# A fused attention and mixture-of-experts block on eight cores: the expert weight loads wait for named tensors of the stage before in place of a fence, and four input loads are recorded earlier

## The chip, the cores and the metric

The kernel runs on the eight cores of one Trainium2 chip. Each core works on one batch element of x (2048 tokens of width 1024) with the same program and its own copy of all weights to read; no core sends anything to another. The metric is the device time of the slowest core in microseconds (us), lower is better.

## The reference, cut to what matters

One layer: x is normalised (layer norm without weights), and three things are added to it: an attention block with its feed-forward part, and a block of eight experts with a router.

```python
xn = layernorm(x)
x = x + attn_block(xn) + expert_block(xn)

def attn_block(x):            # x is xn
    xi = rmsnorm(x @ down_w + down_b, norm1_w)          # 1024 -> 512, two branches of 256
    o1 = branch(xi[..., :256], window=10, shift=5)      # windowed attention, 8 heads each
    o2 = branch(xi[..., 256:], window=20, shift=10)
    x = x + concat(o1, o2) @ up_w + up_b
    h = rmsnorm(x, norm2_w)
    return x + gelu(h @ ffn_w1 + ffn_b1) @ ffn_w2 + ffn_b2   # 1024 -> 2048 -> 1024

def expert_block(t):          # t is xn
    logits = silu(t @ rw1 + rb1) @ rw2 + rb2            # 8 logits
    w = softmax over the two largest logits, 0 elsewhere
    eh = silu(einsum('td,edh->teh', t, ew1) + eb1)      # every expert on every token
    eo = einsum('teh,ehd->ted', eh, ew2) + eb2
    return t + einsum('te,ted->td', w, eo)
```

All eight experts are computed for all tokens: `ew1` is 8 x 1024 x 2048 and `ew2` 8 x 2048 x 1024 in float32, 128 MiB in all, and each core reads all of it.

## The kernel before, in words

**How the order is set.** A class `Prog` (L34) records operations into one list per engine (tensor, vector, scalar, gpsimd, sync). Each operation names the resources (`Res`, L26) it reads and writes, and `op` (L50) derives its semaphore waits from them: a read waits for the tokens of the resource's writers (`w`), a write for those of its writers and of its readers (`rs`). An engine's own list is its order; the order in which operations of different engines are recorded matters only for which tokens exist when a wait is derived. The book-keeping of a write is the part that the change leans on:

```python
for w in wr:
    if w.rs:
        w.w = [tok]
        w.rs = []
    else:
        w.w.append(tok)
```

So a second write of a resource that nobody has read in between waits for the first write, and its token is added to the list. For a DMA the token is its landing: each DMA has a semaphore name (`dma=`) that rises by 16 when it has landed. `fence` (L94) makes the next operation of each engine wait for everything recorded so far on all engines.

**The stages**, each with its own SBUF tensors, opened and closed in turn, so that a later stage's tensors lie where an earlier stage's were:

- P0 (L290 to L362): 16 tiles of 128 tokens of x, each through six small steps `u0` to `u5` (load by SyncE, statistics by VectorE, two ScalarE steps, normalise and start the sum S, eight transposes, copy into XN), recorded in a staggered order by `step` and `sidx` (L354 to L359). The load `u0` (L310) goes to one of four buffers `XST`.
- Router (L364 to L480), attention branches (L482 to L843).
- A4 (L845 to L1034): up projection, norm and feed-forward, two blocks of 512 tokens at a time. `a4_ffn1` (matmuls L962) fills `MID`, `a4_ffn2` (matmuls L987, bias matmul L991) multiplies by `WF2` into PSUM, and VectorE adds the result to the running sum S (L999, L1007). Then comes `P.fence()` (L1032).
- Experts (L1037 to L1133): for each expert e, the weights come as eight DMAs that GpSimd issues, float32 in HBM to bf16 in SBUF, each 1 MiB as it is written: four column quarters of the first matrix into `WE1` (L1066, semaphores `de1` + slot + quarter) and four row quarters of the second into `WE2` (L1071, semaphores `de2` + quarter). `WE1` has two slots (e % 2), `WE2` one. For each block `nt` of 512 tokens, 16 groups of eight matmuls (L1079) make the hidden values, ScalarE applies Silu (L1086) into `EHS`, and for each of four token tiles 16 matmuls `blds_lo` and 16 `blds_hi` (L1098) give the output, which VectorE scales and adds to S (L1116). `blds_lo` reads the quarters 0 and 1 of `WE2`, `blds_hi` 2 and 3. The group m of L1079 reads quarter m // 4 of `WE1`.

`EB2R` is a small tensor (16 KiB) with the experts' output bias; its DMA (L1042) is the first that GpSimd issues after the fence, and the 12 loads of expert 0's `WE1`, `WE2` and of expert 1's `WE1` follow it, with no wait between them. PE reads tokens block by block in order, so nothing of expert 0 past its first `blds_hi` runs before all eight of its loads have landed.

Of the kernel before, what the change touches and what calls it, by code (L numbers as in the profile page):

```python
# [17 lines left out]
NTC = 16  # L18
# [193 lines left out]
def build_nc():  # L212
    nc = bass.Bass("TRN2", target_bir_lowering=False)
    es = ExitStack()
    P = Prog(nc, es)
    t_, v_, s_, g_, y_ = nc.tensor, nc.vector, nc.scalar, nc.gpsimd, nc.sync
# [3 lines left out]
    CN = {}  # L220
# [31 lines left out]
    rFB2R, rEB2R = Res("FB2R"), Res("EB2R")  # L252
# [12 lines left out]
    blk_cm = nc.Block()  # L265
    blk = blk_cm.__enter__()

    for n in CS:
        P.op("sync", (lambda d=CS[n], a=CN[n].ap(): y_.dma_start(d[:, :], a)),
             wr=[rCS[n]], dma="dc_" + n)  # L270
    for n in BRANCH_CONSTS:
        rCS[n] = Res(n)
    P.op("gpsimd", (lambda: g_.dma_start(FB2R[:, :], CN["fb2"].ap())),
         wr=[rFB2R], dma="dcg1")
# [20 lines left out]
    if True:  # L295
        rPT = rPBF
        rXST = [Res(f"XST{i}") for i in range(4)]
        rXNT = [Res(f"XNT{i}") for i in range(4)]
        rMV4 = [Res(f"MV4{i}") for i in range(4)]

        def p0_stages(tc):
            p4 = tc % 4
            p2 = tc % 2
            xs = XST[:, 1024 * p4: 1024 * p4 + 1024]
            xnt = XNT[:, 1024 * p4: 1024 * p4 + 1024]
            mv = MV4[:, 16 * p4: 16 * p4 + 16]
            rmv = rMV4[p4]

            def u0():
                P.op("sync", (lambda tc=tc, xs=xs: y_.dma_start(  # L310
                    xs, xd.ap()[128 * tc: 128 * tc + 128, :])),
                    wr=[rXST[p4]], dma=f"dx{p4}")

            def u1():
                P.op("vector", (lambda: v_.bn_stats(mv[:, 0:6], xs[:, 0:512])),
                     rd=[rXST[p4]], wr=[rmv])
                P.op("vector", (lambda: v_.bn_stats(mv[:, 6:12], xs[:, 512:1024])),
                     rd=[rXST[p4]], wr=[rmv])
                P.op("vector", (lambda: v_.bn_aggr(mv[:, 12:14], mv[:, 0:12])),
                     rd=[rmv], wr=[rmv])  # L320

            def u2():
                P.op("scalar", (lambda: s_.activation(mv[:, 14:15], mv[:, 13:14],
                                                      AF.Ln, bias=CS["epsc"][:, 0:1])),
                     rd=[rmv, rCS["epsc"]], wr=[rmv])
                P.op("scalar", (lambda: s_.activation(mv[:, 15:16], mv[:, 14:15],
                                                      AF.Exp, scale=-0.5)),
                     rd=[rmv], wr=[rmv])

            def u3():  # L330
                P.op("vector", (lambda: v_.tensor_scalar(  # L331
                    xnt, xs, mv[:, 12:13], mv[:, 15:16], ALU.subtract, ALU.mult)),
                    rd=[rXST[p4], rmv], wr=[rXNT[p4]])
                P.op("vector", (lambda tc=tc: v_.tensor_tensor(
                    S[:, 1024 * tc: 1024 * tc + 1024], xs, xnt, ALU.add)),
                    rd=[rXST[p4], rXNT[p4]], wr=[rS[tc]])

            def u4():
                for fc in range(8):
                    P.op("tensor", (lambda fc=fc: t_.transpose(  # L340
                        PT[:, 1024 * p2 + 128 * fc: 1024 * p2 + 128 * fc + 128],
                        xnt[:, 128 * fc: 128 * fc + 128], CS["idb"][:, :])),
                        rd=[rXNT[p4], rCS["idb"]], wr=[rPT[p2]])

            def u5():
                P.op("scalar", (lambda tc=tc: s_.copy(
                    XN3[:, :, 128 * tc: 128 * tc + 128],
                    PT[:, 1024 * p2: 1024 * p2 + 1024].rearrange(
                        "p (c x) -> p c x", c=8))),
                    rd=[rPT[p2]], wr=[rXN4[tc // 4]])  # L350

            return [u0, u1, u2, u3, u4, u5]

        p0s = [p0_stages(tc) for tc in range(NTC)]  # L354
        for step in range(NTC + 5):
            for sidx in range(6):
                t = step - sidx
                if 0 <= t < NTC:
                    p0s[t][sidx]()  # L359
        P.fence()  # L360
        P.replay(blk)
# [123 lines left out]
    if True:  # L485
        rUPIN = [Res(f"UPIN{i}") for i in range(NNT)]
        rWUP = Res("WUP")
# [27 lines left out]
        for n in BRANCH_CONSTS:  # L515
# [3 lines left out]
                 wr=[rCS[n]], dma="dc_" + n)  # L519
        if True:  # L520
# [22 lines left out]
            if True:  # L543
# [17 lines left out]
                for c in range(4):  # L561
                    P.op("vector", (lambda c=c: v_.memset(XI3[:, c, 2048:2052], 0.0)),
                         wr=[rXI])
# [35 lines left out]
            if True:  # L599
# [109 lines left out]
                for br in range(2):  # L709
# [67 lines left out]
                    for step in range(17 + NSTG - 1):  # L777
                        for sidx in range(NSTG):
                            t = step - sidx
# [76 lines left out]
        if True:  # L856
            rH = [Res("H0"), Res("H1")]
            rMID = Res("MID")
            rRST2 = Res("RST2")
            rWF1, rWF2 = Res("WF1"), Res("WF2")  # L860
# [155 lines left out]
            for pr in range(2):  # L1016
# [12 lines left out]
                a4_ffn2(n0)  # L1029
                a4_ffn1(n1)  # L1030
                a4_ffn2(n1)
            P.fence()  # L1032
            P.replay(blk)
        esA4.close()  # L1034
    esU.close()
# [3 lines left out]
    EB2R = esM.enter_context(nc.sbuf_tensor("EB2R", [8, 1024], BF16))  # L1039
    rOST = [Res("OST0"), Res("OST1")]  # L1040
    WE1 = esM.enter_context(nc.sbuf_tensor("WE1", [128, 2 * 8 * 2048], BF16))
    _ = P.op("gpsimd", (lambda: g_.dma_start(EB2R[:, :], CN["eb2"].ap())),  # L1042
             wr=[rEB2R], dma="dcg2")
    WE2 = esM.enter_context(nc.sbuf_tensor("WE2", [128, 16 * 1024], BF16))
    EHS = esM.enter_context(nc.sbuf_tensor("EHS", [128, 16 * 512], BF16))
    PA, PB = Fb(0), Fb(1)
# [2 lines left out]
    if True:  # L1049
        rWE1Q = [[Res(f"we1_{sl}_{q}") for q in range(4)] for sl in range(2)]  # L1050
        rWE2Q = [Res(f"we2_{q}") for q in range(4)]
# [8 lines left out]
        e1hbm = CN["e1w"].ap().rearrange("e (k p) m -> e p k m", p=128)  # L1060
        e2hbm = CN["e2w"].ap().rearrange("e (k p) m -> e p k m", p=128)
        pbanks = [(PA, rPA), (PB, rPB)]
        for e in range(8):
            slot = e % 2
            for q in range(4):
                P.op("gpsimd", (lambda e=e, q=q, slot=slot: g_.dma_start(  # L1066
                    WE13[slot][:, :, 512 * q: 512 * q + 512],
                    e1hbm[e, :, :, 512 * q: 512 * q + 512])),
                    wr=[rWE1Q[slot][q]], dma=f"de1{slot}{q}")
            for q in range(4):  # L1070
                P.op("gpsimd", (lambda e=e, q=q: g_.dma_start(  # L1071
                    WE23[:, 4 * q: 4 * q + 4, :],
                    e2hbm[e, :, 4 * q: 4 * q + 4, :])),
                    wr=[rWE2Q[q]], dma=f"de2{q}")
            for nt in range(NNT):
                for m in range(16):
                    ps, rps = pbanks[m % 2]
# [12 lines left out]
                for tcl in range(4):  # L1090
                    tc = 4 * nt + tcl
# [71 lines left out]
```

How the kernel before makes its waits and increments, by code:

```python
            def body(eng, queue=list(queue), sems=sems):  # L111
                for waits, builders, semname, amt in queue:
                    for s, v in waits:
                        eng.wait_ge(sems[s], v)
                    for b in builders[:-1]:
                        b()
                    builders[-1]().then_inc(sems[semname], amt)
```

## Time and profile before

| | us |
|---|---|
| executions timed | 2946.06 and 3281.86 |
| their median | 3113.96 |
| the profiled execution | 2943.68 |
| its span on the slowest core (core 7) | 2942.1 |
| spans of the eight cores | 2927.9 to 2942.1 |

The median is the midpoint of two executions that lie 335.8 us apart; the profiled execution agrees with the lower of them within 0.1%. The span runs from the first to the last instruction of one core; what the profiled execution has over core 7's span is 1.6 us.

In what follows PE is TensorE's matmul stream, DVE is VectorE, ACT ScalarE, POOL GpSimd, SP SyncE; L987 is line 987 of the kernel before. "Landing" is the time from the start of a DMA's issue to the rise of its semaphore.

### The profile page before, as it was taken

To read this page: it belongs to the slowest core of one execution; us is meant where nothing else is said; L and a number is where in the kernel's file an instruction comes from. 1 tells how busy PE (TensorE), PEld (TensorE's weight loads), DVE (VectorE), ACT (ScalarE), POOL (GpSimd) and SP (SyncE) were. 2 spreads that over 40 slices of the span, in tenths; PEclk is the share of its full clock that TensorE was granted. 3 is DMA by queue.
4 is the path that set the end of the run, shared out by engine and by line. 5 is a ranking of instruction groups with operands and counts; after the bars stand their busy time and mean duration, and the time that the engine had idled before them with its cause. 6 is when DMAs were issued, how large, how long until landed. Compare 5 with 4: busy or idle time off the path is not lost.

```text
span 2942.1 us, 30346 instructions; the slowest of 8 cores (2927.9 to 2942.1 us)
## 1 busy us (share of the span) xinstructions
PE 2557.0 (87%) x11344; PEld 1119.8 (38%) x11344; DVE 559.4 (19%) x699; ACT 627.5 (21%) x966; POOL 61.6 (2%) x80
## 2 busy tenths in 40 slices
PE   3665666666796978999999999999999999999999
PEld 1221332332242333444444444444444444444443
DVE  6012761763214100001001001100100100110001
ACT  2232233231110211211221221121122122112222
POOL 0000000000000010000000000000000000000000
PEclk9986555556796988999999999999999999999999
DMA  5220000005100029007007007006105204303011
GB/s 132 29 45 0 1 1 1 1 1 86 29 1 0 1 32 140 1 1 115 0 1 114 1 1 102 14 1 88 27 1 79 36 1 67 49 1 57 30 44 43
DMA packets 65621, 100.92 MB, mean 34 GB/s; under 512 B 4819, under 2 KB 40148, under 8 KB 65484
## 3 DMA queue, kind: packets, MB, share of 16 engines
q0 software_dynamic: 58080, 80.78, 18.7%
q1 hardware_dynamic: 7404, 18.20, 2.0%
q8 instruction: 100, 1.64, 0.2%
q14 instruction: 37, 0.30, 0.0%
HBM read 171.36 MB, written 8.39 MB: 61 GB/s over the span
## 4 chain that ended last, share of the span: by engine, by line
PE 84%; issue 6%; DVE 4%; DMA 2%; ACT 2%; SPq 0%; another core or an unknown queue 0%; DVEq 0%; POOL 0%; ACTq 0%; POOLq 0%
PE PF L1098 31%; PE PF L1079 29%; PE PF L987 4%; PE PF L962 4%; PE PBF L661 3%; PE PF L676 3%; PE PF L377 2%; DMA WE<-e2w 1%; PE PBF L904 1%; PE PF L618 1%; PE PF L550 1%; PE PF L882 1%; DVE H L951 1%; PE PF L730 1%; PE PF L691 1%
## 5 line engine op out<-in xcount | busy, mean ns | idle before, releaser
L1098 PE MATMUL PF<-WE,EHS 128*128 128x512 bf16 x4096 | 920.1, 380 | 29.6 <-DMA WE<-e2w 10.7
L1079 PE MATMUL PF<-XN,WE 128*128 128x512 bf16 x4096 | 892.0, 380 | 14.7 <-DMA WE<-e1w 14.7
L1086 ACT ACTIVATE EHS<-PF,c_eb1c 128x512 bf16<-128x512 f32 x512 | 351.9, 687 | 1350.3 <-PE PF L1079 1350.3
L1098 PEld LDWEIGHTS PF<-WE,EHS 128*128 128x128 bf16 x4096 | 390.7, 98 | 546.5 <-issue 103.2
L1079 PEld LDWEIGHTS PF<-XN,WE 128*128 128x128 bf16 x4096 | 401.3, 98 | 499.8 <-issue 20.2
L1116 DVE SCALAR_TENSOR_TENSOR S<-PF,WTM,S 128x1024 bf16<-128x1024 f32 x128 | 164.3, 1284 | 1690.3 <-PE PF L1098 1471.3
L661 PE MATMUL PBF<-c_idb,E 120*120 120x120 bf16 (+1 forms) x288 | 91.3, 317 | 52.7 <-DVE E L655 15.1
L962 PE MATMUL PF<-H,WF 128*128 128x512 bf16 x512 | 119.3, 397 | 6.7 <-ACT MID L969 6.7
L987 PE MATMUL PF<-WF,MID 128*128 128x512 bf16 x512 | 116.0, 379 | 3.9 <-ACT MID L969 3.9
L676 PE MATMUL PF<-PTS,VT 120*32 120x120 bf16 x272 | 70.9, 261 | 36.5 <-ACT UPIN L701 1.0
L661 PEld LDWEIGHTS PBF<-c_idb,E 120*120 120x120 bf16 (+1 forms) x288 | 48.6, 169 | 93.1 <-issue 90.7
L962 PEld LDWEIGHTS PF<-H,WF 128*128 128x128 bf16 x512 | 51.4, 101 | 76.1 <-issue 21.6
L340 PE MATMUL PBF<-c_idb,XNT 128*128 128x128 bf16 x128 | 33.7, 264 | 51.2 <-DVE XNT L331 34.5
L377 PE MATMUL PF<-XN,WR 128*128 128x512 bf16 x256 | 57.5, 388 | 19.8 <-DMA WR<-r1w 19.4
L987 PEld LDWEIGHTS PF<-WF,MID 128*128 128x128 bf16 x512 | 47.5, 98 | 65.0 <-issue 12.1
L969 ACT ACTIVATE MID<-PF,c_fb1c 128x512 bf16<-128x512 f32 x64 | 44.0, 687 | 130.9 <-PE PF L962 130.6
L666 ACT COPY PTS<-PBF 120x960 bf16<-120x960 bf16 (+1 forms) x36 | 33.0, 918 | 114.5 <-PE PBF L661 114.5
L676 PEld LDWEIGHTS PF<-PTS,VT 120*32 120x32 bf16 x272 | 27.2, 100 | 77.9 <-issue 74.3
L1071 POOL DMA_DIRECT2D WE<-e2w x32 | 23.9, 756 | 1562.7 <-PE PF L1098 1562.5
L618 PE MATMUL PF<-QKV 32*120 32x120 bf16 x272 | 37.7, 333 | 18.0 <-DVE Z L624 14.4
L624 DVE TENSOR_TENSOR Z<-PF,c_bt 120x960 f32<-120x960 f32 x34 | 39.3, 1156 | 67.3 <-PE PF L618 67.3
L904 PE MATMUL PBF<-c_idb,MID 128*128 128x128 bf16 x128 | 31.3, 257 | 18.9 <-DVE MID L891 2.1
(125 smaller groups left out, 973.3 us busy)
## 6 DMA issues: line engine op xcount, KB each, us to landing
WE<-e1w POOLq DMA_DIRECT2D x32, 1024.0 KB, 41.0
WE<-e2w POOLq DMA_DIRECT2D x32, 1024.0 KB, 20.3
XST<-x SPq DMA_DIRECT2D x16, 512.0 KB, 3.6
out<-OST SPq DMA_DIRECT2D x16, 512.0 KB, 2.6
WF<-f1w POOLq DMA_DIRECT2D x1, 4096.0 KB, 30.7
WF<-f2w POOLq DMA_DIRECT2D x1, 4096.0 KB, 54.2
WR<-r1w POOLq DMA_DIRECT2D x1, 2048.0 KB, 16.7
WDOWN<-dw POOLq DMA_DIRECT2D x1, 1024.0 KB, 12.4
```

The source lines that it names most:

```text
L377: (lambda m=m, nt=nt, k=k, ps=ps: t_.matmul(ps[:, 0:512], WR1[:, 1024 * k + 128 * m: 1024 * k + 128 * m + 128], XN3[:, k, 512 * nt: 512 * ...
L618: P.op("tensor", (lambda h=h, a=a, b=b, nj=nj: t_.matmul(SCP[0:nj, 512 * a + 128 * b: 512 * a + 128 * b + nj], q_ap(h), k_ap(h), start=Tru ...
L661: P.op("tensor", (lambda j=j: t_.transpose(PT[0:nj, 1024 * p2 + 128 * j: 1024 * p2 + 128 * j + nj], E[0:nj, 960 * p4 + nj * j: 960 * p4 + ...
L676: P.op("tensor", (lambda j=j, h=h, a=a, b=b: t_.matmul(PE2[32 * a: 32 * a + 32, 128 * b: 128 * b + nj], vdst[0:nj, 32 * h: 32 * h + 32], P ...
L904: t_.transpose(PT[:, 1024 * pp + 128 * c: 1024 * pp + 128 * c + 128], XA3[:, c, 128 * tcl: 128 * tcl + 128], CS["idb"][:, :])),
L962: (lambda m=m, k=k, ps=ps, hs=hs: t_.matmul(ps[:, 0:512], WF1[:, 2048 * k + 128 * m: 2048 * k + 128 * m + 128], H3[:, k, 512 * hs: 512 * h ...
L969: P.op("scalar", (lambda m=m, ps=ps: s_.activation(MID3[:, m, 0:512], ps[:, 0:512], AF.Gelu, bias=CS["fb1c"][:, m: m + 1])), rd=[rps, rCS[ ...
L987: blds.append(lambda k=k, h2=h2, tcl=tcl, ph=ph: t_.matmul(ph, MID3[:, k, 128 * tcl: 128 * tcl + 128], WF2[:, 1024 * k + 512 * h2: 1024 * ...
L1079: (lambda m=m, nt=nt, k=k, ps=ps, slot=slot: t_.matmul(ps[:, 0:512], WE13[slot][:, k, 128 * m: 128 * m + 128], XN3[:, k, 512 * nt: 512 * n ...
L1086: P.op("scalar", (lambda e=e, m=m, ps=ps: s_.activation(EHS3[:, m, 0:512], ps[:, 0:512], AF.Silu, bias=CS["eb1c"][:, 16 * e + m: 16 * e + ...
L1098: lambda k=k, h2=h2, tcl=tcl, e=e, PEx=PEx: t_.matmul(PEx[0:128, 512 * h2: 512 * h2 + 512], EHS3[:, k, 128 * tcl: 128 * tcl + 128], WE23[: ...
L1116: P.op("vector", (lambda e=e, tc=tc, PEx=PEx: v_.scalar_tensor_tensor(S[:, 1024 * tc: 1024 * tc + 1024], PEx[0:128, 0:1024], WTM[:, 8 * tc ...
```

## The change

Three edits:

1. The four first `u0` of P0 are recorded ahead of the staggered loop, and skipped in it.
2. The fence behind A4 no longer covers GpSimd.
3. In its place, GpSimd's loads name what they overwrite: `alias_a4` lists the resources of A4 whose SBUF the expert stage takes over. The `EB2R` load, moved down to the head of the expert stage, all eight loads of expert 0 and the four `WE1` loads of expert 1 write that list besides their own resource.

```diff
@@ P0
         p0s = [p0_stages(tc) for tc in range(NTC)]
+        for tc in range(4):
+            p0s[tc][0]()
         for step in range(NTC + 5):
             for sidx in range(6):
                 t = step - sidx
-                if 0 <= t < NTC:
+                if 0 <= t < NTC and not (sidx == 0 and t < 4):
                     p0s[t][sidx]()
@@ end of A4
-            P.fence()
+            P.fence(engines=("tensor", "vector", "scalar", "sync"))
             P.replay(blk)
@@ experts
-    _ = P.op("gpsimd", (lambda: g_.dma_start(EB2R[:, :], CN["eb2"].ap())),
-             wr=[rEB2R], dma="dcg2")
...
+        alias_a4 = [rWF1, rWF2, rMID, rH[0], rH[1], rRST2, rWUP] + rUPIN
+        P.op("gpsimd", (lambda: g_.dma_start(EB2R[:, :], CN["eb2"].ap())),
+             wr=[rEB2R] + alias_a4, dma="dcg2")
         for e in range(8):
             slot = e % 2
             for q in range(4):
+                extra = alias_a4 if e < 2 else []
                 P.op("gpsimd", (lambda e=e, q=q, slot=slot: g_.dma_start(
                     WE13[slot][:, :, 512 * q: 512 * q + 512],
                     e1hbm[e, :, :, 512 * q: 512 * q + 512])),
-                    wr=[rWE1Q[slot][q]], dma=f"de1{slot}{q}")
+                    wr=[rWE1Q[slot][q]] + extra, dma=f"de1{slot}{q}")
             for q in range(4):
+                extra = alias_a4 if e == 0 else []
                 P.op("gpsimd", (lambda e=e, q=q: g_.dma_start(
                     WE23[:, 4 * q: 4 * q + 4, :],
                     e2hbm[e, :, 4 * q: 4 * q + 4, :])),
-                    wr=[rWE2Q[q]], dma=f"de2{q}")
+                    wr=[rWE2Q[q]] + extra, dma=f"de2{q}")
```

GpSimd's list at the head of the expert stage, before. The names behind "waits" are semaphores: t, v, s those of the engines' instructions, `dwf1` the load of the first feed-forward matrix, `de20` to `de23` the quarters of `WE2`, `de100` to `de113` those of `WE1` (slot, quarter), `dcg2` the load of `EB2R`.

```order
L1042 DMA EB2R<-eb 8x1024 [waits dwf1,dwf2,s,t,v]
L1066 DMA WE<-e1w 128x8x512 x4
L1071 DMA WE<-e2w 128x4x1024 x4
L1066 DMA WE<-e1w 128x8x512 x4
L1071 DMA WE<-e2w 128x4x1024 [waits de20,t]
```

The same place now (L1067 is the `EB2R` load, L1073 and L1079 the two weight loads there):

```order
L1067 DMA EB2R<-eb 8x1024 [waits dwf1,dwf2,s,t,v]
L1073 DMA WE<-e1w 128x8x512 [waits dcg2]
L1073 DMA WE<-e1w 128x8x512 [waits de100]
L1073 DMA WE<-e1w 128x8x512 [waits de101]
L1073 DMA WE<-e1w 128x8x512 [waits de102]
L1079 DMA WE<-e2w 128x4x1024 [waits de103]
L1079 DMA WE<-e2w 128x4x1024 [waits de20]
L1079 DMA WE<-e2w 128x4x1024 [waits de21]
L1079 DMA WE<-e2w 128x4x1024 [waits de22]
L1073 DMA WE<-e1w 128x8x512 [waits de23]
L1073 DMA WE<-e1w 128x8x512 [waits de110]
```

The order of the loads is the same; each of the 12 now waits for the landing of the one ahead of it.

SyncE's list in P0, before and then now (L310 became L313):

```order
L310 DMA XST<-x 128x1024 x4
L310 DMA XST<-x 128x1024 [waits dx0,v]
L310 DMA XST<-x 128x1024 [waits dx1,v]
L310 DMA XST<-x 128x1024 [waits dx2,v]
L310 DMA XST<-x 128x1024 [waits dx3,v]
```

```order
L313 DMA XST<-x 128x1024 x4
L313 DMA XST<-x 128x1024 [waits dx0,v]
L313 DMA XST<-x 128x1024 [waits dx1,v]
L313 DMA XST<-x 128x1024 [waits dx2,v]
L313 DMA XST<-x 128x1024 [waits dx3,v]
```

Nothing moved there, and on PE, DVE, ACT and SP the lists with their waits are the same before and now in the whole program, but for line numbers; only POOL's differs.

## Rows read from the trace of the kernel before

**Rows 1.** Spans and granted clock of three of the cores

```profile
core 0: 2931.6 us, clock 0.898
...
core 5: 2927.9 us, clock 0.900
...
core 7: 2942.1 us, clock 0.897
```

**Rows 2.** The page: busy time by engine, and the chain that ended last

```profile
PE 2557.0 (87%) x11344; PEld 1119.8 (38%) x11344; DVE 559.4 (19%) x699; ACT 627.5 (21%) x966; POOL 61.6 (2%) x80
...
PE 84%; issue 6%; DVE 4%; DMA 2%; ACT 2%; SPq 0%; another core or an unknown queue 0%; DVEq 0%; POOL 0%; ACTq 0%; POOLq 0%
```

**Rows 3.** Timeline of core 7: start, duration, engine, line, count, [idle before]

```profile
1081.20 0.39 PE L991 MATMUL PF<-FB2R,c_onesb 1*128 1x512 bf16 x1
1081.69 1.49 DVE L1007 TENSOR_TENSOR S<-PF,S 128x512 bf16<-128x512 f32 x2 [6.53 <-PE PF L991]
1083.74 0.54 POOL L1042 DMA_DIRECT2D EB2R<-eb  x1 [388.22 <-DVE S L1007]
1084.27 3.51 POOL L1066 DMA_DIRECT2D WE<-e1w  x4
...
1096.25 30.36 PE L1079 MATMUL PF<-XN,WE 128*128 128x512 bf16 x128 [14.67 <-DMA WE<-e1w]
...
1130.30 6.23 PE L1098 MATMUL PF<-WE,EHS 128*128 128x512 bf16 x16 [3.69 <-DMA WE<-e2w]
...
1143.49 28.11 PE L1098 MATMUL PF<-WE,EHS 128*128 128x512 bf16 x112 [6.96 <-DMA WE<-e2w]
```

**Rows 4.** Core 7 by stretch: length, PE, PEld, DVE, ACT, POOL busy, PEclk, DMA share, GB/s

```profile
1084.00:1096.00 12.00, 0.00 (x0) 0.00 (x0) 0.00 (x0) 0.00 (x0) 10.26 (x13) 0.52 0.79 101
1096.00:1130.00 34.00, 30.36 (x128) 13.08 (x128) 0.00 (x0) 12.28 (x17) 0.00 (x0) 0.90 1.11 157
1130.00:1144.00 14.00, 6.74 (x18) 2.41 (x19) 0.00 (x0) 0.00 (x0) 0.00 (x0) 0.62 1.05 163
1144.00:1150.00 6.00, 6.00 (x18) 2.08 (x17) 0.00 (x0) 0.00 (x0) 0.00 (x0) 0.56 1.13 150
```

**Rows 5.** Timeline of core 7: SyncE issues the loads of x

```profile
12.29 57.10 SPq L310 DMA_DIRECT2D XST<-x  x16
```

**Rows 6.** The chain of work at the hand-over, core 7: start, duration, what

```profile
1083.23 0.51 issue
...
1143.14 0.35 issue
```

**Rows 7.** DMA issues of core 7: queue, count, KB each, median us to landing

```profile
WDOWN<-dw POOLq DMA_DIRECT2D x1, 1024.0 KB, 12.4
...
EB2R<-eb POOLq DMA_DIRECT2D x1, 16.0 KB, 3.5
```

**Rows 8.** Line 1066 (WE1 loads) on core 7, landing times

```profile
DMA to landing us min/median/max: 11.6/41.0/75.2
```

**Rows 9.** Line 1071 (WE2 loads) on core 7, landing times

```profile
DMA to landing us min/median/max: 10.4/20.3/53.2
```

**Rows 10.** Line 1066 on core 0, landing times

```profile
DMA to landing us min/median/max: 8.5/35.5/70.1
```

**Rows 11.** Line 1071 on core 0, landing times

```profile
DMA to landing us min/median/max: 8.2/15.1/48.0
```

**Rows 12.** Core 0 by stretch: length, PE busy, PEclk, DMA share, GB/s

```profile
1086.00:1088.00 2.00, 0.00 (x0) 0.50 1.24 206
...
1094.00:1096.00 2.00, 2.00 (x11) 1.00 1.17 154
```

**Rows 13.** Timeline of core 7: GpSimd's first issue for expert 1

```profile
1337.95 1.50 POOL L1071 DMA_DIRECT2D WE<-e2w  x2 [243.69 <-PE PF L1098]
```

More of the change, by code:

```diff
@@ L266, in build_nc @@
     blk = blk_cm.__enter__()
+    XLD_EARLY = 4
+    _early_xld = []
     for n in CS:
```

## The prediction

> **What bounds the kernel now.** I read the cores first, then the busy shares with the chain of waits, then the timeline of the one place where the change puts its hand. The eight cores end within 0.5% of each other at the same granted clock, so core 7, the slowest, can stand for all [rows 1]. PE is busy 87% of the span and the chain that ended last is 84% PE [rows 2]: a gain or a loss counts only where PE stands still for it. That is so at the hand-over from A4 to the experts [rows 3]: the last bias matmul ends at 1081.59 (1081.20 + 0.39), DVE adds the last tile until 1083.18, GpSimd issues `EB2R` at 1083.74 and then twelve loads without a pause. PE starts expert 0 at 1096.25, its first `blds_lo` at 1130.30 and its first `blds_hi` at 1143.49, and stood idle 14.67, 3.69 and 6.96 us before these, each time for a weight load. From 1143.49 on all eight loads of expert 0 are there and PE works through. So 1143.49 is the moment that the forecast has to move; what follows it is the same work in the same order.
>
> The DMA queue runs without a gap in that stretch: 157 and 163 GB/s at a share of about 1.1 of the engines [rows 4], so of the eight loads each costs only its place in the queue. The first landed 11.6 us after its issue at 1084.27 [rows 3, 8], at 1095.9, and the eighth at 1143.14 [rows 6]: 47.2 us for seven more, 6.75 us apart.
>
> **The change part by part.** *The four loads of x recorded earlier.* They are SyncE's, and SyncE's list has only loads at this place, in the same order and with the same waits before and after (the order shows it). The sixteen issues run from 12.29 for 57.10 us in one stretch [rows 5], behind the small constants, which also keep their place. Price 0; nothing hides it, nothing is changed.
>
> *The fence without GpSimd.* `EB2R` overwrites, by name, tensors that the last `a4_ffn2` reads, so it still waits for the last matmul of A4, but no longer for DVE's last additions. No weight load can start before A4 ends. The gain is the time from 1081.59 to 1083.18, 1.6 us; the 0.51 us from release to issue stays [rows 3, 6]. `EB2R` is then issued at 1082.15.
>
> *The loads' new waits.* Every one of the first twelve loads writes `alias_a4`, no engine reads it in between, so each waits for the token of the last one: the landing. What was one queue of twelve becomes twelve round trips. The first now waits for `EB2R`, 3.5 us from issue to landing [rows 7], which lands at 1085.65; with 0.5 us of release the first weight load is issued at 1086.2, 1.9 us later than before. Then follow eight landings of L each and seven releases of 0.51, and 0.35 us from the last landing to PE [rows 6]. The eighth has been read by PE at 1086.2 + 8 L + 3.6 + 0.35 = 1090.1 + 8 L. Against 1143.49 that is 8 L - 53.4 us.
>
> L is the time of a load that is alone in its core's queue, which the trace shows only at a few places. On core 7 the first `WE1` load took 11.6 [rows 8], the shortest `WE2` load 10.4 [rows 9]. On core 0 they took 8.5 and 8.2 [rows 10, 11]. The upper end is the load of `WDOWN` at the program's start, of the same size and shape as a `WE1` quarter, but beside the loads of constants: 12.4 [rows 7]. What separates the cores is a neighbour's traffic, as I read it: core 0 moved 206 GB/s early on, and 154 from 1094 on [rows 12], when the others were loading too, as core 7's 157 [rows 4]. 1.05 MB take 5.1 us at the one rate and 6.8 at the other; 3.4 (8.5 - 5.1) to 4.8 us (11.6 - 6.8) of a round trip are issue, start and landing, in which nothing moves. In the chain all cores are in this pattern, so a neighbour is moving data in some 63% of the time (6.6 of 10.5 us), and I weigh 10.9, core 7's middle, by 0.63 and core 0's 8.35 by 0.37: L = 10.0 us. The sum is 8 x 10.0 - 53.4 = +26.6 us. The bounds: L = 8.2 gives +12.2, L = 11.6 gives +39.4, L = 12.4 gives +45.8.
>
> The Trainium skill weighs otherwise here (DMA: Bandwidth & Descriptors, Anatomy of one DMA - SWDGE (gpsimd) path): a fixed 2 us a DMA plus its bytes over 436 GB/s. By that a load would be 4.4 us counted as written and 6.8 as read, and the sum -18 or +1 us. The trace disagrees: `EB2R`, with almost no bytes, took 3.5 us, and no 1 MiB load under 8.2. It stays as the rule behind the third rival.
>
> *What the wait holds up behind it.* On GpSimd the waiting loads hold only the further loads. Expert 1's four `WE1` quarters, chained too, land by 1170 + 4 x 10.5 = 1212; PE turns to expert 1 only when expert 0 is done, and GpSimd's first issue for that expert came at 1337.95 [rows 13]: over 120 us of cover, price 0. From expert 2 on no load has the list. Inside expert 0 the first four groups (32 matmuls) of each `WE1` quarter have to fit between two landings. PE's clock was at 0.52 of full speed over the idle stretch and 0.62 and 0.56 after the later waits [rows 4], that is mostly at 1.2 GHz, and 16 matmuls took 6.23 us there [rows 3], 0.39 each. Even if all 32 ran so, 12.5 us, the four quarters would be done at 1097 + 50 = 1147, and `blds_lo`, which waits for the sixth landing at 1086.2 + 6 x 10.5 = 1149, would not be held. The slow clock after the last wait is in both kernels alike: after 1143.49 it was 0.56 for 6 us [rows 4], and it will be so after 1170. Its price is 0.
>
> *The sum.* -1.6 (DVE) + 3.5 (`EB2R` awaited) and the rest of the chain come to +26.6 us at 1143.49, which passes to the end whole, since PE runs without a pause from there. On the profiled execution: 2943.7 + 26.6 = 2970.3 us, 0.9% more. The median of the two runs shown, 3113.96, is the middle of 2946.06 and 3281.86; my sum stands on the lower kind, that of the profiled execution.
>
> **The rivals.**
>
> *A: lone loads at core 0's price.* If the chain thins the traffic so far that neighbours hardly meet, L is 8.2 to 8.5 everywhere: 8 x 8.35 - 53.4 = +13.4, 2957 us. For it: core 0's rows. Against it: the cores end within 14 us of each other [rows 1], so they come to this place nearly together and then all load for 85 us, and the slowest core counts. The Trainium skill (same page, Latency and other measured facts) says that a lighter load on HBM makes a DMA's fixed part smaller, which leans to A; the trace has both cores' landings, but not what of the gap is fixed.
>
> *B: the round trip is dearer than any quiet load.* With L = 12.4, `WDOWN`'s, the sum is +45.8, 2989.5 us. For it: a `WE1` quarter is cut into the same pieces as `WDOWN`, and core 7 had 11.6. Against it: SyncE's loads of constants ran beside `WDOWN`.
>
> *C: faster.* One mechanism: a lone load lands after little more than its bytes take, because its start and landing ran beside other loads in the old queue and were dear for that. At core 0's 206 GB/s, L = 5.1 gives 8 x 5.1 - 53.4 = -12.6, 2931 us. It decides at L = 6.7, below which the change gains. Against it: the first loads had an all but empty queue ahead and still took 8.5 and 11.6 [rows 8, 10].
>
> *D: the change does nothing.* If only the fence and the x loads counted and the chain of waits did not hold PE, the sum would be -1.6 + 0 = 2942 us. Against it: the order has the waits, and PE already stood for these very loads. What is left of D is that L comes out near 6.7.
>
> *E: slower by over 2%.* That wants 59 us, so L = 14. No quiet 1 MiB load took that long; a disturbance of all stages could do it too.
>
> **How the numbers follow.** Forecast (L from 9 to 11.6, +19 to +39) 0.68; A 0.15; B 0.09; C and D together 0.04; E 0.04. The range takes in A and nearly all of B, with the 0.1% by which executions of one kind differ here: 2953 to 2987 us. A measurement of this kernel tells about 2% from no change; all cases but E lie within it, C with its -0.4% too: faster 0.01, same 0.95, slower 0.04.
>
> **What would show it.** In the changed kernel's timeline GpSimd's issues at the hand-over stand apart, about 10.5 us from one to the next, twelve of them, where they were 0.9 apart; the DMA share between them falls below the former 1.1; PE starts expert 0 about 15 us after A4's end as before, then waits before m = 4, 8 and 12, longest before the first `blds_lo` and `blds_hi` (some 10 us and more each), the latter some 89 us after A4's last matmul where it was 62. The landing times of the first twelve loads are all between 8 and 12 us. P0 and the time from the second block of expert 0 to the end keep their lengths (2942.1 - 1143.5 = 1799 us). I am wrong if the loads still go out in one burst, if L is under 8 or over 12, or if the time moved in another stage.

## The result and the profile after

| | before | after |
|---|---|---|
| median of all executions, us | 2944.2 (10) | 2963.6 (11) |
| profiled execution, us | 2943.7 | 2963.0 |
| spans of the cores, us | 2927.9 to 2942.1 | 2954.8 to 2961.4 |

The ratio after to before is 1.0061, with a 95% interval from 1.005 to 1.0072: 18 us slower (15 to 21). In some executions of every kernel here one die or both run at a lower clock and the time is up to 15% longer; the ratios leave these out, and the 3113.96 us shown at first was the midpoint of one such execution and an undisturbed one.

The change did what its waits say. The timeline of the changed kernel at the hand-over, core 3 (its slowest), which answers to [rows 3]; L1067 is the `EB2R` load, L1073 and L1079 the weight loads, L1087 and L1106 the two expert matmuls:

```profile
1081.86 0.39 PE L996 MATMUL PF<-FB2R,c_onesb 1*128 1x512 bf16 x1
1082.36 1.49 DVE L1012 TENSOR_TENSOR S<-PF,S 128x512 bf16<-128x512 f32 x2 [6.53 <-PE PF L996]
1082.87 0.54 POOL L1067 DMA_DIRECT2D EB2R<-eb  x1 [386.68 <-PE PF L996]
1085.56 0.89 POOL L1073 DMA_DIRECT2D WE<-e1w  x1 [2.15 <-DMA EB2R<-eb]
1096.64 9.77 PE L1087 MATMUL PF<-XN,WE 128*128 128x512 bf16 x32 [14.39 <-DMA WE<-e1w]
1096.79 0.87 POOL L1073 DMA_DIRECT2D WE<-e1w  x1 [10.34 <-DMA WE<-e1w]
1107.87 7.07 PE L1087 MATMUL PF<-XN,WE 128*128 128x512 bf16 x32 [1.45 <-DMA WE<-e1w]
...
1117.51 7.07 PE L1087 MATMUL PF<-XN,WE 128*128 128x512 bf16 x32 [2.57 <-DMA WE<-e1w]
...
1127.57 7.07 PE L1087 MATMUL PF<-XN,WE 128*128 128x512 bf16 x32 [2.99 <-DMA WE<-e1w]
1127.75 0.75 POOL L1079 DMA_DIRECT2D WE<-e2w  x1 [9.19 <-DMA WE<-e1w]
...
1145.94 5.57 PE L1106 MATMUL PF<-WE,EHS 128*128 128x512 bf16 x16 [11.31 <-DMA WE<-e2w]
...
1164.38 8.34 PE L1106 MATMUL PF<-WE,EHS 128*128 128x512 bf16 x32 [12.87 <-DMA WE<-e2w]
```

GpSimd now starts `EB2R` 0.6 us after A4's last matmul (1082.25), released by PE and not by DVE; then each issue waits for a DMA, named in the bracket. PE waits not three times but six: the first wait is as long as before (14.39 us), three short ones come in between, and the last two have grown from 3.69 and 6.96 us to 11.31 and 12.87. The waits of the same core in that stretch (who waited for whom: us in total, times, longest):

```profile
POOL WE L1073 <- DMA WE<-e1w: 54.6, 6, 10.4
...
PE PF L1106 <- DMA WE<-e2w: 24.2, 2, 12.9
PE PF L1087 <- DMA WE<-e1w: 21.4, 4, 14.4
```

PE's waits for weights are 45.6 us; before they were 14.67 + 3.69 + 6.96 = 25.3 us on core 7 [rows 3], 20.3 us less. The rate falls with it, where the queue before moved 157 and 163 GB/s [rows 4]. Stretches of the changed kernel's core 3 (columns as in [rows 4]):

```profile
1097.00:1128.00 31.00, 23.98 (x99) 9.88 (x98) 0.00 (x0) 9.53 (x13) 2.66 (x4) 0.92 0.69 102
1128.00:1164.00 36.00, 12.20 (x47) 4.79 (x45) 0.00 (x0) 2.75 (x4) 2.72 (x4) 0.76 0.72 117
```

One figure is used for every kernel below: **the hand-over**, from the end of A4's last bias matmul to the start of expert 0's first `blds_hi`, the moment from which PE is never short of weights. Before it is 61.9 us on core 7 (1143.49 - 1081.59), over the eight cores 55.8 to 61.9, mean 59.5. After it is 82.1 us on core 3 and 76.0 to 82.1 over the cores, mean 78.6. The means differ by 19.1 us, the spans of the slowest cores in the two profiles by 19.3. What follows the hand-over took 1798.1 us on the mean of the cores before and 1797.7 after, so the time came from here. Taken again in a second execution of the same lists, this mean moved by up to 0.9 us (59.5 and 60.2, 78.6 and 77.7 below), and smaller differences of it say nothing.

### The profile page after: what moved, and what is told of

Its sections match the earlier page's. It is cut to its first block, busy times and chain, and to the rows that moved or that the text cites. A ratio compares the mean times of both kernels' runs of the same rounds, so it can differ in the third digit from the quotient of the medians.

```text
span 2961.4 us, 30347 instructions; the slowest of 8 cores (2954.8 to 2961.4 us)
## 1 busy us (share of the span) xinstructions
PE 2555.4 (86%) x11344; PEld 1118.7 (38%) x11344; DVE 559.3 (19%) x699; ACT 627.5 (21%) x966; POOL 61.5 (2%) x80
## 4 chain that ended last, share of the span: by engine, by line
PE 83%; issue 6%; DVE 4%; DMA 4%; ACT 2%; SPq 0%; DVEq 0%; ACTq 0%; POOLq 0%
PE PF L1106 31%; PE PF L1087 29%; PE PF L992 4%; PE PF L967 4%; PE PBF L666 3%; PE PF L681 3%; PE PF L382 2%; DMA WE<-e1w 1%; DMA WE<-e2w 1%; PE PBF L909 1%; PE PF L623 1%; PE PF L555 1%; PE PF L887 1%; DVE H L956 1%; PE PF L735 1%
## 5 line engine op out<-in xcount | busy, mean ns | idle before, releaser
L1106 PE MATMUL PF<-WE,EHS 128*128 128x512 bf16 x4096 | 917.8, 380 | 43.1 <-DMA WE<-e2w 24.2
L1087 PE MATMUL PF<-XN,WE 128*128 128x512 bf16 x4096 | 892.6, 380 | 21.4 <-DMA WE<-e1w 21.4
L1106 PEld LDWEIGHTS PF<-WE,EHS 128*128 128x128 bf16 x4096 | 389.9, 98 | 558.6 <-issue 113.7
L1087 PEld LDWEIGHTS PF<-XN,WE 128*128 128x128 bf16 x4096 | 400.8, 98 | 507.7 <-issue 28.4
L666 PE MATMUL PBF<-c_idb,E 120*120 120x120 bf16 (+1 forms) x288 | 91.3, 317 | 52.7 <-DVE E L660 15.1
L967 PE MATMUL PF<-H,WF 128*128 128x512 bf16 x512 | 119.3, 397 | 6.7 <-ACT MID L974 6.7
L992 PE MATMUL PF<-WF,MID 128*128 128x512 bf16 x512 | 116.0, 379 | 3.9 <-ACT MID L974 3.9
L967 PEld LDWEIGHTS PF<-H,WF 128*128 128x128 bf16 x512 | 51.5, 102 | 76.0 <-issue 21.6
L382 PE MATMUL PF<-XN,WR 128*128 128x512 bf16 x256 | 57.5, 388 | 20.7 <-DMA WR<-r1w 20.3
L992 PEld LDWEIGHTS PF<-WF,MID 128*128 128x128 bf16 x512 | 47.5, 98 | 65.0 <-issue 12.1
L1079 POOL DMA_DIRECT2D WE<-e2w x32 | 23.8, 747 | 1517.7 <-PE PF L1106 1483.0
```

The costliest lines, as they stand in the source:

```text
L382: (lambda m=m, nt=nt, k=k, ps=ps: t_.matmul(ps[:, 0:512], WR1[:, 1024 * k + 128 * m: 1024 * k + 128 * m + 128], XN3[:, k, 512 * nt: 512 * ...
L666: P.op("tensor", (lambda j=j: t_.transpose(PT[0:nj, 1024 * p2 + 128 * j: 1024 * p2 + 128 * j + nj], E[0:nj, 960 * p4 + nj * j: 960 * p4 + ...
L967: (lambda m=m, k=k, ps=ps, hs=hs: t_.matmul(ps[:, 0:512], WF1[:, 2048 * k + 128 * m: 2048 * k + 128 * m + 128], H3[:, k, 512 * hs: 512 * h ...
L992: blds.append(lambda k=k, h2=h2, tcl=tcl, ph=ph: t_.matmul(ph, MID3[:, k, 128 * tcl: 128 * tcl + 128], WF2[:, 1024 * k + 512 * h2: 1024 * ...
L1087: (lambda m=m, nt=nt, k=k, ps=ps, slot=slot: t_.matmul(ps[:, 0:512], WE13[slot][:, k, 128 * m: 128 * m + 128], XN3[:, k, 512 * nt: 512 * n ...
L1106: lambda k=k, h2=h2, tcl=tcl, e=e, PEx=PEx: t_.matmul(PEx[0:128, 512 * h2: 512 * h2 + 512], EHS3[:, k, 128 * tcl: 128 * tcl + 128], WE23[: ...
```

## The experiments

All kernels were compared with the kernel before on the same chip. Ratios are to the kernel before, with 95% intervals.

### The x loads alone

```diff
+        for tc in range(4):
+            p0s[tc][0]()
...
-                if 0 <= t < NTC:
+                if 0 <= t < NTC and not (sidx == 0 and t < 4):
```

> The kernel before with the first edit alone: the four first loads of x recorded ahead of the staggered loop. My theory: SyncE's list is the same in both, so nothing changes; ratio 1.000, and the time from A4's last matmul to expert 0's first blds_hi stays at 62 us. Rival: the earlier recording helps P0 by the 12 us or so that its first tile waits for x; ratio 0.996.

Measured: ratio 0.9998 (0.9988 to 1.0009), hand-over 60.2 us on the mean of the cores. The edit does nothing, as its unchanged list says: to record a load earlier moves it only past operations of its own engine, and SyncE had none in between.

### The list of tensors on EB2R alone

```diff
-                extra = alias_a4 if e < 2 else []
+                extra = []
...
-                extra = alias_a4 if e == 0 else []
+                extra = []
```

> The changed kernel with the list of A4's tensors on the EB2R load alone; the twelve weight loads name only their own quarters, so the wait for A4 is kept (GpSimd issues in order) and the chain of landings is gone. Chain theory: the twelve issues go out in one burst again, and A4's last matmul to first blds_hi is 60 us, 1.6 less than before since DVE's last additions are not awaited; ratio 0.9995. Rival (it is the smaller fence, or the moved EB2R load, that costs): it stays near 80 us and the ratio near 1.006.

Measured: ratio 0.9994 (0.9983 to 1.0005), hand-over 58.1 us on the mean, 1.4 less than before. The burst is back, in this kernel's timeline of core 7:

```profile
1082.21 0.54 POOL L1067 DMA_DIRECT2D EB2R<-eb  x1 [388.76 <-PE PF L996]
1082.74 3.51 POOL L1073 DMA_DIRECT2D WE<-e1w  x4
1086.22 3.01 POOL L1079 DMA_DIRECT2D WE<-e2w  x4
1089.15 3.58 POOL L1073 DMA_DIRECT2D WE<-e1w  x4
```

`EB2R` is issued 0.62 us after A4's last matmul (1081.59), where it was 2.15 before (1083.74). So the smaller fence gains the microsecond and a half that DVE's last additions take (too little for the ratio to tell), and the whole loss is in the chain of landings. The chain theory holds, its rival is out.

### The chain on expert 0 only

```diff
-                extra = alias_a4 if e < 2 else []
+                extra = alias_a4 if e < 1 else []
```

> The changed kernel with the list on expert 0's loads but not on expert 1's four. Cover theory: expert 1's loads are not awaited for over 100 us, so the ratio to the kernel before is 1.006 as for the whole change. Rival (the later loads take bandwidth or delay something): the four now go out in a burst at the end of the chain, and the time differs from the whole change by more than 3 us.

Measured: ratio 1.0067 (1.0047 to 1.0087), hand-over 79.2 us on the mean. The same as the whole change within the intervals: expert 1's chained loads cost nothing, they are covered. The chain of eight loads ahead of `blds_hi` is what is paid.

### Two loads in flight

```diff
+        ring = [Res("ring0"), Res("ring1")]
...
-                extra = alias_a4 if e < 2 else []
+                extra = [ring[q % 2]] if e < 2 else []
...
-                extra = alias_a4 if e == 0 else []
+                extra = [ring[q % 2]] if e == 0 else []
```

> Each of the twelve loads waits for the landing of the one two ahead of it, not one: two in flight. If what the chain costs is the empty time of a round trip (issue, start and landing, some 4 us, in which nothing moves), a second load in flight covers it whole, since a transfer takes 5 to 7 us: A4's last matmul to first blds_hi 60 to 62 us, ratio 0.9995 to 1.000. Rival: waiting on GpSimd itself costs per load (release and issue one after the other), or more loads must be queued for full rate; then half or more of the 18 us remains, 70 us or more, ratio 1.003.

Measured: ratio 0.9992 (0.998 to 1.0004), hand-over 57.3 us on the mean of the cores. One more load in flight takes back the whole loss, and the waits on GpSimd by themselves cost nothing that shows. Its timeline, core 1:

```profile
1102.55 0.88 POOL L1074 DMA_DIRECT2D WE<-e1w  x1 [5.94 <-DMA WE<-e1w]
1109.11 0.75 POOL L1080 DMA_DIRECT2D WE<-e2w  x1 [5.68 <-DMA WE<-e1w]
1115.72 0.74 POOL L1080 DMA_DIRECT2D WE<-e2w  x1 [5.86 <-DMA WE<-e1w]
```

and the stretch from 1095 to 1130 of the same core, at the rate and the DMA share (160 GB/s and 1.11) of the old queue:

```profile
1095.00:1130.00 35.00, 31.13 (x133) 13.40 (x134) 0.00 (x0) 12.28 (x17) 4.63 (x6) 0.93 1.11 160
```

The issues are 6.6 us apart, as the landings were in the kernel before (6.75).

### The chained loads in halves

The same bytes in 16 round trips ahead of `blds_hi`.

```diff
-                    WE13[slot][:, :, 512 * q: 512 * q + 512],
-                    e1hbm[e, :, :, 512 * q: 512 * q + 512])),
+                        WE13[slot][:, ks, 512 * q: 512 * q + 512],
+                        e1hbm[e, :, ks, 512 * q: 512 * q + 512])),
...
-                    WE23[:, 4 * q: 4 * q + 4, :],
-                    e2hbm[e, :, 4 * q: 4 * q + 4, :])),
+                        WE23[:, ks, :],
+                        e2hbm[e, :, ks, :])),
```

Here `ks` runs over the two halves of the rows of each quarter.

> The changed kernel with each of the twelve chained loads cut into two chained halves (the same bytes, 16 round trips ahead of expert 0's first blds_hi in place of 8). A lone load is taken as a + bytes / rate. With the 8.8 us that the changed kernel shows for 1 MiB and 206 GB/s, a is 3.7, a half takes 6.2 and with the release 6.7: 16 x 6.7 = 108 where 8 took 74, so A4's last matmul to first blds_hi grows from 82 to 115 us and the ratio to the kernel before is 1.018. Rival (the skill's fixed 2 us, the rest being a slower transfer): 16 x 5.9 = 94, 102 us, ratio 1.013. Rival 2 (time goes by bytes alone): 82 us, ratio 1.006.

Measured: ratio 1.0124 (1.0108 to 1.014), hand-over 96.9 to 100.3 us, mean 98.9. Each trip costs, so it is not bytes alone (rival 2 is out); but it costs much less than the 115 us of my split of L, and a little less than the rival's 102. In the timeline of core 7 the issues are 5.8 us apart:

```profile
1135.79 0.70 POOL L1084 DMA_DIRECT2D WE<-e2w  x1 [6.00 <-DMA WE<-e1w]
1141.54 0.71 POOL L1084 DMA_DIRECT2D WE<-e2w  x1 [5.05 <-DMA WE<-e2w]
1147.36 0.70 POOL L1084 DMA_DIRECT2D WE<-e2w  x1 [5.12 <-DMA WE<-e2w]
```

### EB2R behind the chain

```diff
-        P.op("gpsimd", (lambda: g_.dma_start(EB2R[:, :], CN["eb2"].ap())),
-             wr=[rEB2R] + alias_a4, dma="dcg2")
         for e in range(8):
             slot = e % 2
+            if e == 2:
+                P.op("gpsimd", (lambda: g_.dma_start(EB2R[:, :], CN["eb2"].ap())),
+                     wr=[rEB2R], dma="dcg2")
```

> The changed kernel with the EB2R load moved behind expert 1's loads; the first weight load takes the wait for A4 itself. The chain of eight starts some 2.7 to 3.5 us sooner: A4's last matmul to first blds_hi 79 us, ratio to the kernel before 1.005. Rival (PE waits for something else at the start): no difference from the whole change.

Measured: ratio 1.0044 (1.0024 to 1.0065), hand-over 74.9 us on the mean, 3.7 less than in the whole change (2.8 less than its repeat below): the landing of a 16 KiB load, awaited, was part of the bill, and the rival is out. The first weight load now starts 0.6 us after A4's last matmul (1082.39 on core 0) and waits for PE alone:

```profile
1082.99 0.88 POOL L1074 DMA_DIRECT2D WE<-e1w  x1 [386.71 <-PE PF L996]
1092.98 0.87 POOL L1074 DMA_DIRECT2D WE<-e1w  x1 [9.12 <-DMA WE<-e1w]
```

With the `EB2R` load ahead of it, it started 3.6 us after A4's last matmul on the mean of the cores.

### The changed kernel again

> The changed kernel once more, beside the three others on the same chip: ratio 1.006 to the kernel before, A4's last matmul to first blds_hi 80 to 83 us, lone landings 8.2 to 11.3 us.

Measured: ratio 1.0066 (1.0044 to 1.0087), hand-over 76.1 to 79.9 us, mean 77.7, below the 80 to 83 that I expected; that was the slowest core's 82.1 of the first execution taken for all. The eight loads ahead of `blds_hi` landed after 8.1 to 10.3 us.

### The chained loads in pairs

```diff
-            for q in range(4):
-                extra = alias_a4 if e < 2 else []
+            nq = 2 if e < 2 else 1
+            for q in range(0, 4, nq):
+                extra = alias_a4 if e < 2 else []
...
-                    WE13[slot][:, :, 512 * q: 512 * q + 512],
-                    e1hbm[e, :, :, 512 * q: 512 * q + 512])),
-                    wr=[rWE1Q[slot][q]] + extra, dma=f"de1{slot}{q}")
+                    WE13[slot][:, :, 512 * q: 512 * (q + nq)],
+                    e1hbm[e, :, :, 512 * q: 512 * (q + nq)])),
+                    wr=rWE1Q[slot][q:q + nq] + extra, dma=f"de1{slot}{q}")
```

and the same for expert 0's `WE2`.

> The changed kernel with its chained loads joined in pairs, 2 MiB written each: four round trips ahead of expert 0's first blds_hi in place of eight. From core 7's period of 9.2 us for 1 MiB and 5.84 for the halves: a trip costs 2.5 + 6.7 per MiB (release in it). Fixed part theory: 15.9 us a trip, A4's last matmul to first blds_hi 3.6 + 4 x 15.9 = 67 us, ratio to the kernel before 1.002. Rival (my prediction's split: 3.7 + 0.5 fixed and 5.1 per MiB, the neighbours hardly meeting): 14.4 us a trip, 61 us, ratio 1.000. Rival 2 (neighbours meet more as the idle part shrinks, 6.8 per MiB and 4.2 fixed): 17.8 us, 75 us, ratio 1.0045.

Measured: ratio 1.0031 (1.0019 to 1.0042), hand-over 62.9 to 70.4 us, mean 65.9. The fixed-part theory's 67 is nearest, rival 1 (61) and rival 2 (75) lie outside the mean by 5 and 9 us. The ratio is a little above its 1.002. Issues on core 7 stand 15.1 and 15.8 us apart:

```profile
1113.64 0.87 POOL L1081 DMA_DIRECT2D WE<-e2w  x1 [14.33 <-DMA WE<-e1w]
1128.78 0.87 POOL L1081 DMA_DIRECT2D WE<-e2w  x1 [14.27 <-DMA WE<-e2w]
1144.55 0.87 POOL L1074 DMA_DIRECT2D WE<-e1w  x1 [14.89 <-DMA WE<-e2w]
```

The mean time from one issue to the next, over the trips ahead of `blds_hi` and over the eight cores, is 5.98 us for 0.5 MiB, 9.39 for 1 MiB (the changed kernel) and 15.64 for 2 MiB; 0.53 us of each is the release, from a landing to the next issue. From the first pair: 6.8 us per MiB and 2.6 fixed, from the second 6.2 and 3.2. So a round trip costs about 3 us besides its bytes, the release in it, and each further MiB costs about the 6.75 us of the full queue.

### Loads that start while A4 still runs

This version lays the expert tensors out again, so that what is free first is filled first, and waits for the users of just those bytes. The waits come as reads of a resource that holds copies of tokens, so no load waits for another.

```diff
+    EB2R = esM.enter_context(nc.sbuf_tensor("EB2R", [8, 1024], BF16))
+    WE1A = esM.enter_context(nc.sbuf_tensor("WE1A", [128, 8 * 2048], BF16))
     OST = esM.enter_context(nc.sbuf_tensor("OST", [128, 2 * 1024], F32))
-    EB2R = esM.enter_context(nc.sbuf_tensor("EB2R", [8, 1024], BF16))
-    WE1 = esM.enter_context(nc.sbuf_tensor("WE1", [128, 2 * 8 * 2048], BF16))
-    WE2 = esM.enter_context(nc.sbuf_tensor("WE2", [128, 16 * 1024], BF16))
     EHS = esM.enter_context(nc.sbuf_tensor("EHS", [128, 16 * 512], BF16))
+    WE2 = esM.enter_context(nc.sbuf_tensor("WE2", [128, 16 * 1024], BF16))
+    WE1B = esM.enter_context(nc.sbuf_tensor("WE1B", [128, 8 * 2048], BF16))
...
+        def gone(*rs):
+            g = Res()
+            for r in rs:
+                g.w += r.w + r.rs
+            return [g]
+        free_lo = gone(rWUP, rH[0], rH[1], *rUPIN)
+        free_wf1 = gone(rRST2, rWF1)
+        free_hi = gone(rWF1, rWF2, rMID)
...
-             wr=[rEB2R] + alias_a4, dma="dcg2")
+             rd=free_lo, wr=[rEB2R], dma="dcg2")
...
-                extra = alias_a4 if e < 2 else []
+                extra = [free_lo, free_hi][e] if e < 2 else []
...
-                    wr=[rWE1Q[slot][q]] + extra, dma=f"de1{slot}{q}")
+                    rd=extra, wr=[rWE1Q[slot][q]], dma=f"de1{slot}{q}")
...
-                extra = alias_a4 if e == 0 else []
+                extra = free_wf1 if e == 0 else []
...
-                    wr=[rWE2Q[q]] + extra, dma=f"de2{q}")
+                    rd=extra, wr=[rWE2Q[q]], dma=f"de2{q}")
```

> A version meant to beat both. The expert tensors are laid out so that WE1's first slot and EB2R lie where UPIN, WUP and H were, WE2 where RST2 and WF1 were, and the second slot over WF1's end and WF2; each load waits for the instructions that used just these tensors and for no other load. All but the second slot are free when A4's last a4_ffn1 ends, 31.5 us before A4's end. EB2R goes out at 1050.6, the eighth load lands by 1051.2 + 11.6 + 47.3 = 1110.1, PE starts expert 0 right behind DVE's last additions at 1083.3 and its blds_hi at 1115 without a wait and with the clock up. A4's last matmul to first blds_hi: 33 us where it was 62; with 3 us less of slow matmuls behind it 32 us gained, ratio 0.989. Rival: the early loads slow A4's last matmuls or land later for the neighbours' loads, and half the gain is lost, 0.994.

Measured: ratio 0.9904 (0.9886 to 0.9921), median 2916.7 us. Its timeline, core 6 (L967 is A4's first feed-forward matmul, L992 and L996 the second one and its bias, L1081 and L1087 the loads, L1095 and L1114 the expert matmuls):

```profile
1050.77 0.55 POOL L1075 DMA_DIRECT2D EB2R<-eb  x1 [355.19 <-PE PF L967]
...
1051.30 3.52 POOL L1081 DMA_DIRECT2D WE1A<-e1w  x4
...
1054.78 3.02 POOL L1087 DMA_DIRECT2D WE<-e2w  x4
1055.04 3.63 PE L992 MATMUL PF<-WF,MID 128*128 128x512 bf16 x16
...
1081.86 0.39 PE L996 MATMUL PF<-FB2R,c_onesb 1*128 1x512 bf16 x1
1082.79 3.52 POOL L1081 DMA_DIRECT2D WE1B<-e1w  x4 [25.00 <-PE PF L996]
1083.99 29.47 PE L1095 MATMUL PF<-XN,WE1A 128*128 128x512 bf16 x125 [1.74 <-DVE S L1012]
...
1113.30 3.62 PE L1114 MATMUL PF<-WE,EHS 128*128 128x512 bf16 x16
1117.06 7.07 PE L1114 MATMUL PF<-WE,EHS 128*128 128x512 bf16 x31
```

GpSimd is released by the last matmul of `a4_ffn1`, eight loads go out 31 us before A4's end, and no core has a wait of PE for a DMA left at the hand-over. A4's matmuls beside the loads keep their 3.63 us per 16. `blds_hi` begins behind the 3.6 us of `blds_lo`, at 1117: 34.8 us after A4's end (1082.25), on every core, where the mean was 59.5. That is 1.8 us behind the 33 that I expected, and it makes 24.7 us on the mean of the cores; what follows took 1795.8 us in place of 1798.1. The granted clock was 1.00 in the first 6 us of it (1117 to 1123, core 6), where it had been 0.56 on core 7 before [rows 4]. Together these are 27 us, where I had expected 32, reckoned from core 7's 61.9; the rival's half is out. The new layout and the waits on few tensors were not tried apart. The same kernel once more:

> The early version once more, beside the one without TensorE's fence: ratio to the kernel before 0.990, no DMA wait of PE between A4 and expert 0.

Measured: ratio 0.992 (0.9898 to 0.9943), median 2916.7 us of ten executions; on no core does PE wait for a DMA there.

### The same, with TensorE out of the fence

```diff
-            P.fence(engines=("tensor", "vector", "scalar", "sync"))
+            P.fence(engines=("vector", "scalar", "sync"))
```

> The version with the early loads, with TensorE left out of the fence behind A4 as well: expert 0's first matmuls write banks that their own resources guard, and read the weights and XN. PE no longer waits 1.7 us for DVE's last additions: A4's last matmul to expert 0's first matmul 0.1 us where the early version had 1.8, ratio to the kernel before 0.9898. Rival: the first weight load's landing or the table load on ScalarE holds PE there anyway, no gain over the early version (0.9904).

Measured: ratio 0.9899 (0.9882 to 0.9915), median 2914.8 us. The intervals of the two versions overlap. The hand-over is 32.1 us on every core, where it was 34.8 and, the second time, 34.5 on the mean. In the timeline the wait of 1.74 us is gone, core 0:

```profile
1081.68 0.39 PE L996 MATMUL PF<-FB2R,c_onesb 1*128 1x512 bf16 x1
1082.00 3.63 PE L1095 MATMUL PF<-XN,WE1A 128*128 128x512 bf16 x16
...
1084.04 1.28 ACT L1102 ACT_TABLE_LOAD   x1 [33.29 <-PE PF L1095]
...
1086.27 24.33 PE L1095 MATMUL PF<-XN,WE1A 128*128 128x512 bf16 x112 [0.65 <-ACT EHS L1102]
```

PE goes from A4 to expert 0 without a pause, and then stands 0.65 us for ScalarE, whose first Silu waits for its table load of 1.28 us. (That wait of 0.65 us was there in the version with the fence too, on some cores.) This is the fastest kernel of the study by its median, 1% below the one before and 1.6% below the changed one; its last edit shows in the hand-over, but whether it adds to the early loads in the total stays open at this precision.

## Why the prediction was right or wrong

**Where the time would be decided: right.** The hand-over carries the difference (19.1 us on the mean of the cores, 19.3 between the slowest cores' spans), and everything behind it kept its length (1798.1 and 1797.7 us).

**The x loads, price 0: right** (ratio 0.9998).

**The fence without GpSimd, -1.6 us: right in kind and size.** `EB2R` was issued 2.2 us after A4's last matmul before and 0.6 after it now, and with the chain taken out the hand-over fell by 1.4 us on the mean.

**Eight round trips in place of eight places in a queue: right.** Without the chain the loss is gone (0.9994), with it on expert 0 alone it is all there (1.0067). The cover for expert 1's loads held, and so did the cover for the slow matmuls: on every core PE still had to wait for the load ahead of `blds_lo`, by 9 us or more in the changed kernel.

**L, the time of one lone load: the term that was mis-sized.** I put L at 10.0 us, and the sum at +26.6. Over the eight cores a chained load took 8.86 us from issue to landing (9.39 from issue to issue), and by my own formula 8 x 8.86 - 53.4 = +17.5 us. The formula itself held: on core 7, from whose rows it was made, L was 8.70, the sum by it is +16.2, and its hand-over grew from 61.9 to 78.3 us, by 16.3. The L of 8.86 lies below the 9 to 11.6 on which the forecast's chance of 0.68 stood, and nearer to rival A (8.35, +13.4, chance 0.15) than to my 10.0; that 2963.6 fell in the range of 2953 to 2987 is owed to the range having taken in A. The step that failed is the sentence that weighed core 7's contended landings by the share of time in which a neighbour moves data: 0.63 of 10.9 and 0.37 of 8.35. With these two values the measured L asks for a weight of 0.2. The periods of the changed kernel's core 3 were 11.2 and 11.3 us for the first two loads, as I had assumed, then 9.6, 10.1, 9.2, 9.4, 9.0 and 9.2; on the cores 0, 1 and 5 none of the first three was over 9.6. A mid-chain load on core 7 in half-microsecond steps (POOL busy, clock, DMA share, GB/s), issued at 1134.00:

```profile
1134.50:1135.00 0.50, 0.24 (x1) 1.00 0.00 0
...
1135.50:1136.00 0.50, 0.00 (x0) 1.00 1.50 45
...
1137.00:1137.50 0.50, 0.00 (x0) 0.86 1.05 168
...
1139.50:1140.00 0.50, 0.00 (x0) 0.50 1.12 213
...
1141.50:1142.00 0.50, 0.00 (x0) 0.50 0.51 90
...
1142.50:1143.00 0.50, 0.00 (x0) 0.50 0.00 0
```

It moves nothing for a microsecond, then little until 1136.5, climbs to 213 GB/s where the full queue had 157 on the mean [rows 4], and has nothing left to move from 1142.5, 0.8 us before the next issue at 1143.31. Steps so short scatter (in the full queue of the same core, from 1100 to 1120, they went from 111 to 199); but over the 64 loads of all cores ahead of `blds_hi` the middle half of the bytes moved at 201 GB/s on the mean, near the 206 of core 0 with little beside it [rows 12]. So neighbours slowed the chained loads far less than the full queues slow one another. Why is open: that the cores fall out of step, so that their transfers seldom meet, would explain it, but the times of different cores are not on one scale in the profile, and this was not shown.

**`EB2R`, 3.5 us: right for core 7 alone.** The same trace has the row of core 0:

```profile
EB2R<-eb POOLq DMA_DIRECT2D x1, 16.0 KB, 2.0
```

In the changed kernel it took 3.4 us on the cores 5 and 7 and 2.0 to 2.5 on the other six, 2.5 on the mean, so that the chain of these six started 1.0 to 1.5 us sooner than my sum has it.

**The split of L: wrong, without harm to the sum.** I read 3.4 to 4.8 us of a trip as fixed. Halves and pairs give 2.6 to 3.2 with the release, 2.1 to 2.7 without, and 6.2 to 6.8 us a MiB. Part of what I had taken as fixed grows with the load. The middle half of a load's bytes moved at 205, 201 and 193 GB/s for 0.5, 1 and 2 MiB; at these rates the bytes take 2.6, 5.2 and 10.9 us of landing times of 5.45, 8.86 and 15.1, and 2.9, 3.6 and 4.2 us are left for the start, the climb and the end.

The Trainium skill puts the fixed part of a DMA at about 2 us (DMA: Bandwidth & Descriptors, Anatomy of one DMA - SWDGE (gpsimd) path). I had set that aside on the 3.5 us of `EB2R`, but the 2.1 to 2.7 us of the runs and core 0's 2.0 us for `EB2R` agree with it. Its other term, the bytes over 436 GB/s, does not come out here: an estimate by it for a MiB written, two read, is 4.8 us, and a MiB took 6.2 or more.

**The direction.** I forecast 0.9% more, not to be told from no change at 2%; with ten and eleven executions it came out as 0.6% more, clear of noise. The 2970.3 us has to be read against 2943.7: against the 3113.96 us shown at first it would look like a gain of 4.6%, and the kernel got slower. Rival A came nearest, as said; B to E did not happen; C, that a lone load costs only its bytes, is refuted by the halves.

## What to carry to other kernels

A wait that names "everything that lies where I write" has to be given to each load as a wait on the old users only; if the loads are recorded as writers of the same resource, each waits for the landing of the one before it, and a queue of eight 1 MiB loads at 6.75 us each becomes eight trips at 9.4. Where the loads have to be held back, two in flight were enough here to hide it all, and loads twice as large hid part (hand-over 65.9 us in place of 78.6).

Dropping a fence gains only what the fence awaited beyond the true dependence, here 1.5 us; the 27 us came from loads that wait for few tensors and lie where these are free early. Put what is loaded first over what dies first, and a stage's weights arrive under the tail of the stage before.

## What the runs showed of the hardware that I had not expected

- Chained lone loads moved the middle half of their bytes at 201 GB/s on the mean, where core 7's full queue moved 157 to 163 [rows 4], with all eight cores in the same pattern. The DMA share of core 3 over the stretch was 0.69 to 0.72 where core 7's full queue had 1.11.
- Two 1 MiB loads in flight per core are a full queue: 160 GB/s, the same as twelve.
- The ten waits of GpSimd, six of them ahead of `blds_hi`, added nothing that could be seen when a second load was in flight (hand-over 57.3 us against 58.1 for the burst with the same start).
- The landing of a 16 KiB load took 2.0 us on some cores and 3.4 to 3.5 on others, in the same execution.
